# Second cross attention of a two-layer decoder: the residual is added by a product on TensorE and copied out by ScalarE, in place of an add on VectorE

## What is computed

```
def _L1_xattn_ref(x, cond, Wq, bq, Wkv, bkv, Wp, bp):
    q = (x @ Wq + bq).reshape(1, B * N, H, hd)
    kv = (cond @ Wkv + bkv).reshape(1, -1, 2, H, hd)
    ...
    q = _fq_sym(q, axis=-1)
    k = _fq_sym(k, axis=-1)
    v = _fq_sym(v, axis=2)
    attn = jnp.einsum('bhqd,bhkd->bhqk', q, k)
    attn = jax.nn.softmax(attn.astype(jnp.float32), axis=-1)
    attn = _fq_unsigned(attn, axis=-1)
    out = jnp.einsum('bhqk,bhkd->bhqd', attn, v)
    out = jnp.transpose(out, (0, 2, 1, 3)).reshape(B, N, C)
    return out @ Wp + bp
...
x = x + _L1_xattn_ref(_layernorm(x, axis=-1), ctx_2048, ...)
x = x + _L1_ffn_ref(_layernorm(x, axis=-1), ...)
```

## Time and profile before

| | |
|---|---|
| three runs | 1347.7, 1354.45, 1354.82 us; median 1354.45 |
| profiled execution | 1352.21 us, of which 1350.5 us are the span from the first to the last instruction |
| mean granted TensorE clock | 0.918 of 2.4 GHz |
| busy share of the span | PE 84%, DVE 68%, ACT 47%, POOL 43% |
| scores of the second cross attention | 256 products, from 768.9 to 1092.9 us of the span |
| adds of L1930 | 16, at 813.6 to 1108.0 us |

### The profile page before, as it was taken

One profiled execution on the slowest core, in us unless ns is written; L12 is line 12 of the kernel. 1 busy time (PEld: TensorE's weight loads), 2 busy tenths in 40 slices (PEclk: granted clock), 3 DMA queues, 4 the chain that ended last, 5 costly groups with the idle time before them and its releaser, 6 DMA issues.

```text
span 1350.5 us, 26395 instructions
## 1 busy us (share of the span) xinstructions
PE 1132.2 (84%) x8459; PEld 874.8 (65%) x8459; DVE 924.0 (68%) x2493; ACT 635.6 (47%) x1431; POOL 580.3 (43%) x869
## 2 busy tenths in 40 slices
PE   3699988994899999767888677887878878999998
PEld 2476766773899999645666355555555554787855
DVE  5575773676344444587788499999999864655657
ACT  3164654331221221324556498988889851433310
POOL 6143543256322222352446354466655653455510
PEclk8799999997899999977899889978889778999999
DMA  5875843212211111254462300000000014455555
GB/s 133 201 210 143 211 120 112 81 52 103 77 48 48 48 52 49 71 151 121 115 155 56 130 1 1 10 25 34 31 20 25 26 41 137 124 160 151 155 183 152
DMA packets 75957, 127.09 MB, mean 94 GB/s; under 512 B 11847, under 2 KB 59335, under 8 KB 72423
## 3 DMA queue, kind: packets, MB, share of 16 engines
q1 hardware_dynamic: 62286, 95.00, 25.8%
q0 software_dynamic: 10272, 28.39, 5.8%
q10 hardware_dynamic: 3264, 2.01, 0.5%
HBM read 76.84 MB, written 48.13 MB: 93 GB/s over the span
## 4 chain that ended last, share of the span: by engine, by line
PE 50%; issue 20%; ACT 9%; POOL 7%; DVE 7%; DMA 4%; ACTq 1%; SPq 1%; another core or an unknown queue 0%; POOLq 0%; DVEq 0%
PE ps L229 12%; PE ps L1216 10%; PE ps L1203 8%; ACT work L1961 5%; PE ps L1187 5%; POOL work L1995 4%; PE ps L483 3%; DMA W<-work 2%; PE ps L1172 2%; DVE work L611 2%; PE ps L496 2%; PE ps L465 1%; POOL xs_scratch L1551 1%; ACTq L741 1%; ACT work L1966 1%
## 5 line engine op out<-in xcount | busy, mean ns | idle before, releaser
L1567 POOL DMA_INDIRECT ys_scratch<-work x118 | 120.5, 1021 | 249.9 <-DVE work L1405 116.2
L1961 ACT ACTIVATE work<-ps,work 128x512 f32<-128x512 f32 x256 | 205.5, 824 | 40.8 <-POOL work L1995 39.6
L1899 DVE TENSOR_REDUCE work<-ps 128x1 f32<-128x512 f32 x256 | 172.0, 678 | 15.4 <-PE ps L1806 15.2
L611 DVE TENSOR_REDUCE work<-ps 128x2 f32<-128x512 f32 (+1 forms) x192 | 127.5, 685 | 75.4 <-PE ps L465 74.1
L794 POOL TENSOR_SCALAR_AFFINE_SELECT work<-work 128x256 f32<-128x256 f32 (+1 forms) x192 | 92.8, 488 | 170.7 <-ACT work L725 169.2
L1995 POOL TENSOR_SCALAR work<-work 128x1 f32<-128x1 f32 x256 | 100.3, 392 | 127.7 <-DVE work L1899 112.7
L1216 PE MATMUL ps<-work,SM 128*128 128x128 f32 x1248 | 147.5, 277 | 0.3 <-issue 0.3
L1216 PEld LDWEIGHTS ps<-work,SM 128*128 128x128 f32 x1248 | 144.2, 194 | 0.7 <-issue 0.7
L725 ACT ACTIVATE work<-ps 128x512 f32<-128x512 f32 x192 | 110.3, 598 | 61.2 <-PE ps L483 60.7
L1806 PE MATMUL ps<-SM,work 128*128 128x512 bf16 x256 | 106.6, 418 | 38.0 <-ACT work L1961 33.0
L1203 PE MATMUL ps<-W,work 128*128 x470 | 121.1, 380 | 0.0
(11 more groups left out here) (265 smaller groups left out, 2519.7 us busy)
## 6 DMA issues: line engine op xcount, KB each, us to landing
work<-xs_scratch SPq DMA_DIRECT2D x79, 132.0 KB
W<-ys_scratch SPq DMA_DIRECT2D x16, 512.0 KB
q_parts<-work SPq DMA_DIRECT2D x48, 128.0 KB, 1.8
W<-in_w_in SPq DMA_DIRECT2D x6, 1024.0 KB, 11.4
W<-q_parts SPq DMA_DIRECT2D x15, 384.0 KB
work<-xs_scratch SPq DMA_DIRECT2D x39, 130.0 KB
W<-k_parts SPq DMA_DIRECT2D x8, 512.0 KB
W<-in_w_out SPq DMA_DIRECT2D x1, 4096.0 KB, 19.1
```

What stands on the lines that cost most here:

```text
L611: q.e.tensor_reduce(self.m[:, j, h0:h0 + n], ov, AX, ALU.max).then_inc(*up("mx", L, b, u))
L1567: q.e.indirect_dma_start(YS[L], bass.IndirectOffsetOnAxis(ap=self.dst[n % self.NY], axis=0), self.YB[n % self.NY], None).then_inc(*landing ...
L1899: q.e.tensor_reduce(self.mm[:, h:h + 1], PS[banks.of["c1_s", t, h]][:, :], AX, ALU.max, negate=True).then_inc(*up("c1_mx", t, h))
L1961: q.e.activation(self.ee[n // 2 % 3][:, 512 * (h % 2):512 * (h % 2) + 512], PS[banks.of["c1_s", t, h]][:, :], ACT.Exp, bias=self.nb[:, h:h ...
```

## The change

The sum `x + OnT' wp1` is now made in PSUM: TensorE first multiplies the identity `idf` with x of the tile (`start=True`), then adds the two products onto it. `pe_o` is written out with three pieces in place of two, so it lies at heads 4, 5 and 6. The first piece waits for `c1_xb` (the bias add of GpSimd) and the bank; the second for `OnT` and the weights. ScalarE copies the bank to x at head 7, behind its exponential, and raises `x_c1`. VectorE's add is gone.

```
             def pe_o(self, q, t):
                 bk, free = banks.take(self.r1, ("c1_o", t), [("x_c1", t)])
-                q.wait_ge(at("c1_OnT", t), at("c1_wp", 1), *free)
-                yield from self.halves(q, PS[bk], [(self.OnT[:, k, :], wp1[:, k, :]) for k in range(2)], "c1_o", t)
+                q.wait_ge(at("c1_xb", t), *free)
+                q.e.matmul(PS[bk][:, 0:256], idf[:, :], x[:, t, :], start=True, stop=False, skip_group_check=True)
+                yield
+                q.wait_ge(at("c1_OnT", t), at("c1_wp", 1))
+                q.e.matmul(PS[bk][:, 0:256], self.OnT[:, 0, :], wp1[:, 0, :], start=False, stop=False, skip_group_check=True)
+                yield
+                q.e.matmul(PS[bk][:, 0:256], self.OnT[:, 1, :], wp1[:, 1, :], start=False, stop=True, skip_group_check=True).then_inc(
+                    *up("c1_o", t))
...
-                    if h == 7 and 2 <= t < T + 2:
-                        q.wait_ge(at("c1_o", t - 2), at("c1_xb", t - 2))
-                        e.tensor_tensor(x[:, t - 2, :], x[:, t - 2, :], PS[banks.of["c1_o", t - 2]][:, 0:256], ALU.add).then_inc(*up("x_c1", t - 2))
...
+                    if h == 7 and 2 <= t < T + 2:
+                        q.wait_ge(at("c1_o", t - 2))
+                        q.e.copy(x[:, t - 2, :], PS[banks.of["c1_o", t - 2]][:, 0:256]).then_inc(*up("x_c1", t - 2))
```

## The result

The changed kernel takes 1346.25 us in the median of 20 runs, the kernel before 1352.65 us in the median of 20. The ratio is 0.9956, with a 95% interval from 0.9938 to 0.9975, so the change saves 0.44%, about 6 us. Two repetitions on other occasions gave 0.9960 [0.9940, 0.9979] and 0.9952 [0.9926, 0.9978]. The runs of either kernel spread over 12 to 17 us, much more than the change moves them, and a single execution says little: the profiled one had 1341.36 us (span 1339.6), 10.9 us less in the span than the one before, and 3.8 us of those had already passed when the second cross attention began (its first scores start at 765.1 instead of 768.9 us), in code that is the same in both.

The account below looks back on a forecast made before the run. VectorE was taken to bound the second cross attention, the other engines waiting for it. From 1353.3 us, less 4.7 for the adds, plus 1.3 for the last two tiles, the forecast was 1349.9 us, range 1343.6 to 1358.5.

Parts of the forecast that it names:

- The ring with VectorE at its head: Second cross attention, 800 to 1084 us: GpSimd, ScalarE and TensorE all end up waiting for VectorE, which waits only 9.1 us.
- VectorE's add, 14 x 0.335: Full stretch of the second cross attention: removing 14 adds saves their pitch of 0.335 us each, 4.7 us.
- ScalarE's copy at nothing: Head 7: the new copy's 0.25 us fits ScalarE's idle time at heads 7 and 8; 3.5 us without that cover.
- The identity products at nothing in the stretch: Heads 4 to 6: TensorE's idle time hides 14 added products of 0.43 us; 6.0 us without that cover.
- The last two tiles, +1.3 us: Tiles 14 and 15, TensorE unhidden at 1.2 GHz: added products cost 0.4 and 0.9 us, together 1.3 us more.
- The page's cost formula: VectorE from PSUM: 120 cycles plus one per element at 0.96 GHz, 0.39 us an add; 5.5 us saved, sum 1349.1.
- Rival D: TensorE's clock between 1026 and 1031 us: higher load holds it up, saving 7 x 1.7 = 11.9 us, 1338.0; chance 0.14.
- What would show it: Two-tile period down about 0.7 us, ScalarE idle some 0.4 and 0.0, VectorE's score waits near 9, tail up 1.3 us.
- the 1 us that would have been called wrong: Sign against the forecast: a two-tile period that doesn't fall, or falls by over 1 us.

Follow-up runs that it names:

- the two other parts alone: TensorE's part and ScalarE's part, each made by itself without the rest of the change: ratios 1.0010 and 0.9988 to the kernel before.
- the mirror: Kernel before with every add on VectorE made twice, the first into unused memory: ratio 1.0079 to the kernel before.
- the last two tiles alone: The change made for tiles 14 and 15 only, tiles 0 to 13 added by VectorE as before: ratio 0.9997 to the kernel before.
- TensorE's part: Identity product as in the change, but VectorE instead of ScalarE copies the sum from PSUM to x: ratio 1.0010 to the kernel before.
- ScalarE's part: Kernel before, add still on VectorE, with 14 extra unused 128x256 copies from PSUM on ScalarE: ratio 0.9988 to the kernel before.

## Why the prediction was right

The forecast was 1349.9 us, 3.4 us or 0.25% below the point it started from, within a range of 1343.6 to 1358.5; measured are 1346.25 us and, by the ratio, 0.44% (about 6 us). It named "no change by measurement, with a lean to faster", and the result is inside the 0.5%; 20 runs of each kernel were enough to hold it clear of 1, which the forecast didn't count on. The mechanism was right and the gain was undersized by some 2.5 us.

- *What bounds the stage.* The ring with VectorE at its head was right. Taking 0.54 us a pair from VectorE took 0.51 from P and 0.57 from Q, adding 0.67 added 0.68 and 0.67, and the two other parts alone added nothing to either.
- *VectorE's add, 14 x 0.335.* Per pair 0.67 was forecast, and the undisturbed pair gives 0.70, 0.74 and 0.69 in the three profiles of the change. P gives more, 0.82, 0.95 and 0.94, for two reasons. In the two repetitions the last tile that P counts is 1 us shorter and the next one 1.8 us longer than in the first profile, so some 0.2 of their P is a shift at its edge: the same distance taken on VectorE from the fifth to the fifteenth multiplication, divided by five, falls from 41.84 to 40.98, 41.06 and 41.07. The rest, 0.1 or so a pair, is that the longer pairs were less long or fewer. For 7 pairs this makes 5.4 to 6.0 us instead of 4.7: this term was undersized by about 1 us.
- *ScalarE's copy at nothing.* Right, with the idle time left behind it as forecast in one tile (0.41 against "some 0.4").
- *The identity products at nothing in the stretch.* Right; a second one would in the mean not have been free.
- *The last two tiles, +1.3 us.* At the clock of 0.50 that I assumed it is 1.13 us, of which tile 15 has 0.91 (forecast 0.9) and tile 14 0.22 (forecast 0.4). What I had left out is that this clock level is not fixed there: it rose on the way in the first profile of the change, and in two profiles with the old last tiles too. With both risen the difference is 0.15 us (0.27 where the last two tiles alone are changed: 8.04 us). The term belongs in the sum with a spread.
- *What the sum leaves open.* From stretch and end together the three profiles of the change are 6.9, 4.6 and 4.3 us better than the profile of before, and the totals 6, 5.4 and 6.5 us. The size agrees; a closer account isn't possible, since the total also varies outside the stage.
- *The page's cost formula* (the Trainium skill, VectorE: DVE Perf Modes, section on the TRN2 errata) would have given 0.39 us an add. Its estimate is near the record (0.41), but the record is not what the period pays: the mirror paid 0.34.
- *Rival D*, the clock held up by more load, gave 1338.0. The granted clock from 800 to 1084 us is 0.89 before and after. That part falls. Its reading of the rows was off in two points: the clock falls twice in this pair of tiles, not once (from 1005.7 to 1012 and from 1026.1 to 1029.5), and at 1026.1 it fell as the 0.66 us of idle time began, behind a wait of 1.47 us ahead of the scores at 1025.69. The absence of pairs of 42.5 us and more could be a small piece of it; see the last section.
- *What would show it* came mostly as written: the clock and VectorE's 9.1 us of waiting stayed, and the period fell, by 0.82 to 0.95 in P rather than 0.7 and so not far from the 1 us that would have been called wrong. The end of the stage went the other way in the first profile.

## What to carry to other kernels

On an engine that is busy without gaps, price an instruction by the distance between the starts of its neighbours, not by its record: here 0.33 against 0.41 us for an add, and 0.06 against 0.15 for a tiny one. Before moving work to another engine, look where that engine stands idle in the round, not how busy it is in the mean: ScalarE at 88% took one copy for nothing at the head where it had caught up, and a second one lengthened the period in the mean. Where a stage's period varies, compare its undisturbed periods as well as its mean. Measure a stage by its own period where the total of one kernel varies by more than the change is worth.

## What the hardware showed that I had not expected

The total of one and the same kernel varies by about 1%, and much of it is made outside the stage: of the 12.0 us between the first and the second profile of the change, 11.1 had passed before the first scores of the second cross attention (765.1 and 776.2 us), while P stays within 0.13 us.

TensorE's clock falls to 1.2 GHz once in nearly every tile of the stretch, in every profile. As a rule it costs little: the undisturbed pair of 40.87 us holds two such falls. What counts is when it falls. Four of the tiles that P covers, in all fourteen profiles, take over 22 us (22.06, 22.19, 22.59 and 22.96; the last two tiles alone, TensorE's part, ScalarE's part, and the second profile with two identity products). They are the four in which the clock fell between 0.9 us ahead of the transposed output that the tile is counted from and 4.6 us behind it, where the dense part of the round begins; in the others it fell 1.7 to 6.6 us ahead (two had no fall). The change has none of these four, but neither has the kernel before, whose pair of 42.57 us holds a tile of 21.15 in place of some 20.5. Whether the change's shorter period keeps the clock's falls in place or these are three lucky profiles, I can't tell; it would need many profiles of both kernels. The Trainium skill, TensorE: Matmul & The Clock Gate, Part 1, says that the throttled state is the default and activity releases it. The rows agree as far as the clock falls behind idle time (1.73 us of waiting ahead of the 0.57), but more products, in one of the two profiles with two identity products, came with such a tile rather than without.
